# Turning R back by transposes under the query bias, and the sums of x3 taken with its addition

## The chip, the cores and the metric

The program runs on one NeuronCore of a Trainium2 chip. The metric is the device time of one execution in microseconds (us). Engines are named as the profile does: PE is TensorE's matmul stream and PEld its weight loads, DVE is VectorE, ACT is ScalarE, POOL is GpSimd, SP is SyncE (here it issues the DMAs).

## What is computed

The input x has 8 images of 128 x 128 pixels with 32 channels, fp32. Four layers follow each other, each added to its input, each behind a group norm in which every channel of every image is a group of its own:

```python
x = x + _L0_conv_ref(_gn(x), w1, wg, w2)        # per-channel expansion, gelu, 32x32 mixes, gelu, weighting
x = x + _L1_conv_ref(_gn(x), fir)               # 4x4 blur
x = x + _L2_conv_ref(_gn(x), W_qk, b_qk, temp)  # window attention, 8x8 windows
x = x + _L3_conv_ref(_gn(x), W1, b1, gamma, beta)  # involution 3x3, batch norm, leaky relu
```

The change is at the end of the third layer and in the statistics that the fourth one needs:

```python
q = q.reshape(B, WS, H1, WS, W1, HEADS, N)    # queries: a linear map of the window's pixels, N = 64 places
k = k.reshape(B, WS, H1, WS, W1, HEADS, ck)   # keys: 8 channels for each of 4 heads
attn = jnp.einsum('bxyhcp,bxyhdp->bxyhcd', q, k) * temperature   # per window and head: 64 x 8
# attn is laid out again as an 8 x 8 window of 32 channels and added to x (this gives x3)
m = jnp.mean(g, axis=(1, 2, 4)); s = jnp.var(g, axis=(1, 2, 4))  # _gn's moments of x3
```

## The kernel before

The 8 images are worked in two sets of 4 (`NS = 2`), since 4 images x 32 channels fill the 128 partitions. A set's pixels lie in `X` as 128 x 16384 (column w major, row h minor). Each set goes through stages 1 to 4 in turn (the four layers' work up to the moments of x3), then stage 5 follows for the last set and the output for both. At every stage's end `stage_end` makes all five engines wait for each other. The order on each engine's queue is written out by hand, with semaphores between engines.

Stage 4 is the one that changes. Its input is `mall`, the attention matrices M of every window, from stage 3. A *duo* is two columns of windows (16 x 128 pixels of the set, `DUOS = 8` per set), and takes four PSUM banks of 512 columns:

- `r_sum(i)` (L624, TensorE): R, the sum over the input channels of query weights times M, for duo i, into banks 0 to 3. It waits until ScalarE has copied the R of the duo before (`s_rc`).
- the copies (L798, ScalarE): banks 0 to 3 go to `rs[:, i % 2]` in SBUF by two ACTIVATEs of 1024 columns, each raising `s_rc`.
- `r_back(i)` (TensorE): in each of the banks 4 to 7, a product of 32 rows puts down the query bias times the key sums (L646, opens the sum), and four 128 x 128 products of `rs` with the identity turn R back onto it, so that channels are on partitions (L651). Each bank raises `s_xt`. Before it writes bank b of duo i, it waits until VectorE has added that bank of the duo before (`s_x3`).
- VectorE (L1102): `X += bank`, one tensor_tensor for each of the four banks, raising `s_x3`; then `bn_stats` of the same 512 columns (L1093), two per window column.

TensorE's order is `r_sum(0)`, `turn_keys()`, then for every i `r_sum(i + 1)`, `r_back(i)`. `turn_keys` (L632) and two copies by VectorE (L1082) make ready the key sums for the bias. After the last duo VectorE merges the 32 sets of statistics (`moments`, L853 and L854), and GpSimd makes the coefficients of the next group norm from `mv` (L1204 to L1207) and scales the tap weights with them (L1281, L1282), which TensorE's next products (L404, L407) need. On ScalarE a one-column Gelu (L801) stands at the end of the first set's stage. GpSimd does nothing else in stage 4.

## Time and profile before

| | us |
|---|---|
| median of 3 runs (897.27 to 901.45) | 898.84 |
| the profiled execution | 900.62 |
| its span, first to last instruction | 898.7 |
| TensorE matmuls busy | 687.2 (76%) |
| TensorE weight loads busy | 467.2 (52%) |
| VectorE busy | 606.9 (68%) |
| ScalarE busy | 505.4 (56%) |
| GpSimd busy | 265.6 (30%) |
| stage 4 of the first set, first R sum to GpSimd's coefficients | 313.5 to 371.5 |
| stage 4 of the second set | 663.7 to 721.2 |

Busy times overlap, since the engines run side by side, and an engine's idle time costs nothing unless others wait for it. So the table says which engines have room, and the rows by stage say who waits for whom. The granted clock is TensorE's: its two levels are 1.2 and 2.4 GHz, and 1.00 in a row means the upper one throughout.

### The profile page before, as it was taken

Reading aid. Unit: us, or ns where it says so; the run is one execution under the profiler, and the core shown is the slowest. Engines: PE = TensorE matmul, PEld = TensorE weight load, DVE = VectorE, ACT = ScalarE, POOL = GpSimd, SP = SyncE. Lnnn points to the kernel's source line nnn. Section 1 sums busy time; section 2 is a strip of 40 time slices with the busy share of each in tenths; the row PEclk is TensorE's granted clock in tenths of the full one; section 3 lists DMA queues with packets and bytes.
Section 4 is the critical chain, followed back from the end, with each engine's and each line's share of the span. In section 5 each row is a group of like instructions: output and inputs, shape, how many; then the busy total and the mean of one; then the engine's idle time right before and its main releaser. Section 6 shows DMA issues by size and latency. Waiting matters only on the chain. (4 is left out here: it accounts for less than half of the span.)

```text
span 898.7 us, 23273 instructions
## 1 busy us (share of the span) xinstructions
PE 687.2 (76%) x9840; PEld 467.2 (52%) x9840; DVE 606.9 (68%) x1117; ACT 505.4 (56%) x500; POOL 265.6 (30%) x301
## 2 busy tenths in 40 slices
PE   5477776499688799799988659968879988436674
PEld 5322222199666488656311159956658787113443
DVE  4557776699844367556699889954437845968861
ACT  4799999234265433388899614436623100635875
POOL 4511110464055400000000067126510000637863
PEclk9789999799899999899999969979989979657987
DMA  9432220000000000000000000000000000001778
GB/s 307 140 92 83 75 83 25 1 1 1 1 3 4 4 3 2 1 2 1 25 2 1 1 1 2 2 2 3 4 3 3 1 25 1 0 0 51 236 216 246
DMA packets 59910, 37.18 MB, mean 41 GB/s; under 512 B 1952, under 2 KB 59424, under 8 KB 59808
## 3 DMA queue, kind: packets, MB, share of 16 engines
q1 hardware_dynamic: 59808, 35.71, 13.2%
q8 instruction: 78, 1.28, 0.6%
q14 instruction: 24, 0.20, 0.1%
HBM read 18.93 MB, written 16.78 MB: 40 GB/s over the span
## 5 line engine op out<-in xcount | busy, mean ns | idle before, releaser
L728 ACT ACTIVATE work<-X,l0s 128x2048 f32<-128x2048 f32 (+2 forms) x80 | 138.5, 1762 | 16.6 <-POOLq L305 16.6
L743 ACT ACTIVATE work<-ps 128x2048 f32<-128x2048 f32 x64 | 121.0, 1890 | 20.8 <-PE ps L437 20.7
L437 PE MATMUL ps<-work,cst 32*32 32x512 f32 x2048 | 74.3, 606 | 38.5 <-ACT work L743 26.4
L762 ACT ACTIVATE work<-ps 128x512 f32<-128x512 f32 x80 | 47.8, 597 | 92.7 <-PE ps L514 92.7
L525 PE MATMUL ps<-cst,work 128*128 128x143 f32 x640 | 94.8, 293 | 0.4 <-DVE X L1009 0.4
L1204 POOL TENSOR_TENSOR co<-mv,cst 128x1 f32<-128x1 f32 x7 | 1.3, 191 | 317.1 <-DVEq L305 264.3
L525 PEld LDWEIGHTS ps<-cst,work 128*128 128x128 f32 x640 | 86.2, 196 | 1.1 <-issue 1.0
L930 DVE TENSOR_TENSOR X<-X,ps 128x512 f32<-128x512 f32 x64 | 43.7, 683 | 58.3 <-PE ps L450 58.2
L450 PE MATMUL ps<-work,w2d 128*32 128x512 f32 x512 | 70.4, 618 | 2.2 <-ACT work L743 2.2
L798 ACT ACTIVATE work<-ps 128x1024 f32<-128x1024 f32 x32 | 31.0, 1021 | 70.4 <-PE ps L624 70.4
L407 PEld LDWEIGHTS ps<-cst,X 128*128 128x128 f32 x512 | 63.7, 207 | 10.1 <-issue 10.1
L323 POOL TENSOR_SCALAR work<-X,co 128x2048 f32<-128x2048 f32 (+1 forms) x16 | 62.8, 3939 | 20.2 <-PE ps L514 19.8
L1306 POOL TENSOR_TENSOR work<-X,work 128x1024 f32<-128x1024 f32 (+1 forms) x32 | 60.6, 1918 | 21.2 <-ACT work L822 21.2
L514 PE MATMUL ps<-cst,work 128*128 128x128 f32 x320 | 51.0, 284 | 19.7 <-DVE work L1032 19.7
L407 PE MATMUL ps<-cst,X 128*128 128x108 f32 x512 | 65.9, 290 | 0.0
L780 ACT ACTIVATE work<-ps 128x520 f32<-128x520 f32 x64 | 38.7, 605 | 47.1 <-PE ps L574 47.0
L651 PEld LDWEIGHTS ps<-cst,work 128*128 128x128 f32 x512 | 58.4, 192 | 12.1 <-ACT work L798 9.1
L651 PE MATMUL ps<-cst,work 128*128 128x128 f32 x512 | 61.4, 278 | 0.0
L1048 DVE TENSOR_SCALAR work<-X,co 128x1024 f32<-128x1024 f32 x32 | 38.2, 1205 | 33.4 <-PE ps L558 29.6
L1102 DVE TENSOR_TENSOR X<-X,ps 128x512 f32<-128x512 f32 x64 | 42.3, 682 | 24.2 <-PE ps L651 24.2
L1270 POOL TENSOR_TENSOR work<-cst,work 128x256 f32<-128x256 f32 x64 | 58.6, 916 | 0.0
L574 PE MATMUL ps<-work 64*64 64x65 f32 x2048 | 48.7, 229 | 12.3 <-ACT work L780 11.0
(130 smaller groups left out, 1288.5 us busy)
## 6 DMA issues: line engine op xcount, KB each, us to landing
out<-work SPq DMA_DIRECT2D x64, 256.0 KB, 3.2
work<-x SPq DMA_DIRECT2D x16, 512.0 KB, 6.0
work<-x SPq DMA_DIRECT2D x32, 256.0 KB, 2.9
work<-choose SPq DMA_DIRECT2D x8, 128.0 KB, 2.6
cst<-consts SPq DMA_DIRECT2D x1, 1009.5 KB, 9.7
cst<-consts SPq DMA_DIRECT2D x1, 64.0 KB, 1.9
```

Source lines behind the costliest of these rows:

```text
L323: eng.tensor_scalar(strip[:, u, :, lo:hi].rearrange("p h w -> p w h"), X3[:, ds(s * W + t * OW + (lo - 1), hi - lo), :], rstd, nmr, ALU.mu ...
L407: o = pe.matmul(ps[:, 6 + t % 2, j * G * K9:(j + WIDE) * G * K9], X[:, f * PIX + w * H:f * PIX + (w + 1) * H], w9s.rearrange("p (o k) -> p ...
L437: last = pe.matmul(ps[C * m:C * m + C, g, :], wg[rows, m, C * g:C * g + C], y_piece(i, j, m)[rows, :], start=True, stop=True)
L450: last = pe.matmul(ps[C * g:C * g + C, 4 + k % 2, :], w2d[:, :], zb[:, k % ZDEEP, g, :], start=True, stop=True)
L514: last = pe.transpose(ps[:, q, k * P:k * P + P], rows.rearrange("p h w -> p (h w)"), ident)
L525: last = pe.matmul(ps[:, DEEP + 2 * (q % 2) + par, at:at + OW * OH], patch[:, q, k, :], c("fir"), start=True, stop=True)
L574: last = pe.matmul(ps[2 * C * pair:2 * C * pair + 2 * C, 2 + hp, pp * HALF:(pp + 1) * HALF], both[:, 0:2 * C], both, start=True, stop=True)
L651: last = pe.matmul(ps[:, 4 + b, q * P:q * P + P], rs[:, i % RING, 4 * b + q, :], ident, start=False, stop=(q == 3))
L728: act.activation(o, x_in.rearrange("p (j n) -> p j n", n=BANK), ACT.Gelu, scale=l0s[:, at:at + 1], bias=l0s[:, at + MULTI:at + MULTI + 1]) ...
L743: act.activation(zb[:, k % ZDEEP, :, :], ps[:, 0:4, :], ACT.Gelu).then_inc(s_zs, 1)
L1270: pool.tensor_tensor(dx[:, n % SLOTS, :, :, :].rearrange("p a b k -> p (a b) k"), eye, sums.rearrange("p a b o -> p (a b) o").broadcast_to ...
L1306: pool.tensor_tensor(y, group_columns(s, j, b, n), y, ALU.add).then_inc(s_fo, 1)
```

## The change

In `r_back` the transposes come first and open the sum: R is turned by matmuls with `is_transpose=True`, whose output is laid out within a bank by window column j, then window, then row i, so that it matches X's order. The query bias comes second, as the product that closes the sum, with its moving operand in the same order. The four banks are done as two pairs (transposes of two banks, then biases of two banks), and each pair waits for its own copy by ScalarE. VectorE adds a bank with a scalar_tensor_tensor that writes the row sums of the new x3 to `sums`, and its bn_stats are dropped. ScalarE squares x3 minus the mean of x2 (`minus_mean`), 1024 columns at a time, one window column each, and writes the row sums of the squares to `squares`; the squares themselves go to a scratch (`squared`). Each square waits for VectorE's two additions and for the square before it. In ScalarE's order the two squares of duo i - 1 stand behind the copies of duo i, and the last two at the end. At the stage's end `totals` replaces the merge of the statistics: two reductions and four small steps on VectorE give mean and variance. Nothing of the computation is left out.

```diff
--- before.py
+++ after.py
@@ -105,6 +105,7 @@
         w2d = sb("w2d", C)
         head_of, place_of = sb("head_of", HEADS), sb("place_of", WS)
         tap = sb("tap", 2 * G * K9)
+        sums, squares, tot = sb("sums", NB), sb("squares", NB), sb("tot", 4)
         ps = ctx.enter_context(nc.psum_tensor("ps", [P, 8, BANK], fp32))
 
         X3 = X[:, :].rearrange("p (w h) -> p w h", h=H)
@@ -177,6 +178,8 @@
         bias_q, _e = part(_e, [WS, N])
         ksum = work[:, _e:_e + NWIN * NWIN]
         assert _e + 2 * NWIN * NWIN <= WORK
+        squared = work[:, _e + NWIN * NWIN:_e + NWIN * NWIN + 2 * BANK]
+        assert _e + NWIN * NWIN + 2 * BANK <= WORK
 
         U, _e = part(0, [3, W, G])
         T, _e = part(_e, [TB + 2, G * K9])
@@ -266,6 +269,8 @@
         s_rc = sem("r_copied")
         s_xt = sem("r_transposed")
         s_x3 = sem("x3_written")
+        s_sq = sem("squares_summed")
+        s_tot = sem("total_step")
         s_sel = sem("sel_loaded")
         s_sc = sem("s_spread")
         s_v = [rsem("even_v_ready", "dve"), rsem("odd_v_ready", "pool")]
@@ -639,18 +644,20 @@
                     if i == 0:
                         pe.wait_ge(s_bq, s + 1)
                         pe.wait_ge(s_kl, s + 1)
-                    for b in range(4):
-                        if nn:
-                            pe.wait_ge(s_x3, 4 * nn - 3 + b)
-                        rows = slice(C * b, C * b + C)
-                        pe.matmul(ps[:, 4 + b, :], turned_k[rows, i, :], bias_q[rows, :, :].rearrange("p w n -> p (w n)"),
-                                  start=True, stop=False)
-                    pe.wait_ge(s_rc, 2 * nn + 2)
-                    for b in range(4):
-                        for q in range(4):
-                            last = pe.matmul(ps[:, 4 + b, q * P:q * P + P], rs[:, i % RING, 4 * b + q, :], ident,
-                                             start=False, stop=(q == 3))
-                        last.then_inc(s_xt, 1)
+                    for pair in range(2):
+                        pe.wait_ge(s_rc, 2 * nn + pair + 1)
+                        for b in range(2 * pair, 2 * pair + 2):
+                            if nn:
+                                pe.wait_ge(s_x3, 4 * nn - 3 + b)
+                            by_pixel = ps[:, 4 + b, :].rearrange("p (j q i) -> p q j i", j=WS, i=WS)
+                            for q in range(4):
+                                pe.matmul(by_pixel[:, 2 * q:2 * q + 2, :, :], rs[:, i % RING, 4 * b + q, :], ident,
+                                          start=(q == 0), stop=False, is_transpose=True)
+                        for b in range(2 * pair, 2 * pair + 2):
+                            rows = slice(C * b, C * b + C)
+                            pe.matmul(ps[:, 4 + b, :], turned_k[rows, i, :],
+                                      bias_q[rows, :, :].rearrange("p w (j i) -> p j w i", j=WS),
+                                      start=False, stop=True).then_inc(s_xt, 1)
 
                 r_sum(0)
                 turn_keys()
@@ -789,6 +796,15 @@
                 stage_end(act, s, 3)
 
 
+                def square_x3(w1):
+
+                    at = s * PIX + w1 * WS * H
+                    act.wait_ge(s_x3, s * NB + 2 * w1 + 2)
+                    if w1:
+                        act.wait_ge(s_sq, s * NWIN + w1)
+                    act.activation(squared, X[:, at:at + WS * H], ACT.Square, bias=minus_mean,
+                                   accum_out=squares[:, w1:w1 + 1]).then_inc(s_sq, 1)
+
                 for i in range(DUOS):
                     nn = s * DUOS + i
                     act.wait_ge(s_r, nn + 1)
@@ -797,6 +813,11 @@
                     for j in range(0, 4, 2):
                         act.activation(rs[:, i % RING, 4 * j:4 * j + 8, :].rearrange("p m k -> p (m k)"),
                                        ps[:, j:j + 2, :].rearrange("p j k -> p (j k)"), ACT.Copy).then_inc(s_rc, 1)
+                    if i:
+                        square_x3(2 * i - 2)
+                        square_x3(2 * i - 1)
+                square_x3(NWIN - 2)
+                square_x3(NWIN - 1)
                 if s + 1 < NS:
                     act.activation(warm[:, 1:2], warm[:, 0:1], ACT.Gelu)
                 stage_end(act, s, 4)
@@ -852,6 +873,29 @@
             def moments(n):
                 dve.drain()
                 dve.bn_aggr(mv[:, :], stats[:, 0:6 * n]).then_inc(s_aggr, 1)
+
+            steps_t = [0]
+
+            def totals(n1, n2, minus_c):
+
+                def step(ins):
+                    ins.then_inc(s_tot, 1)
+                    steps_t[0] += 1
+
+                def stepped():
+                    dve.wait_ge(s_tot, steps_t[0])
+                    alone(dve)
+
+                step(dve.tensor_reduce(tot[:, 0:1], sums[:, 0:n1], mybir.AxisListType.X, ALU.add))
+                step(dve.tensor_reduce(tot[:, 1:2], squares[:, 0:n2], mybir.AxisListType.X, ALU.add))
+                stepped()
+                dve.tensor_scalar(mv[:, 0:1], tot[:, 0:1], 1.0 / PIX, None, ALU.mult)
+                step(dve.tensor_scalar(tot[:, 2:3], tot[:, 0:1], 1.0 / PIX, minus_c, ALU.mult, ALU.add))
+                stepped()
+                step(dve.tensor_tensor(tot[:, 3:4], tot[:, 2:3], tot[:, 2:3], ALU.mult))
+                stepped()
+                dve.scalar_tensor_tensor(mv[:, 1:2], tot[:, 1:2], 1.0 / PIX, tot[:, 3:4], ALU.mult, ALU.subtract
+                                         ).then_inc(s_aggr, 1)
 
             dve.wait_ge(s_ident, 16)
             by_head = ident.rearrange("p (g h k) -> p h g k", g=G, h=HEADS)
@@ -1087,22 +1131,15 @@
                     def half_windows(hf):
                         return X3[:, ds(s * W + w1 * WS, WS), 64 * hf:64 * hf + 64]
 
-                    def measure_x3(hf):
-                        dve.wait_ge(s_x3, s * NB + w1 * 2 + hf + 1)
-                        alone(dve)
-                        dve.bn_stats(stats[:, 12 * w1 + 6 * hf:12 * w1 + 6 * hf + 6], half_windows(hf))
-
-                    def windows(hf):
-                        return half_windows(hf).rearrange("p j (q i) -> p j q i", i=WS)
-
-
                     for hf in range(2):
                         dve.wait_ge(s_xt, s * NB + w1 * 2 + hf + 1)
-                        src = ps[:, 4 + 2 * (w1 % 2) + hf, :].rearrange("p (q j i) -> p j q i", j=WS, i=WS)
-                        dve.tensor_tensor(windows(hf), windows(hf), src, ALU.add).then_inc(s_x3, 1)
-                    measure_x3(0)
-                    measure_x3(1)
-                moments(NB)
+                        v = half_windows(hf)
+                        dve.scalar_tensor_tensor(v, v, 1.0, ps[:, 4 + 2 * (w1 % 2) + hf, :].rearrange("p (j h) -> p j h", j=WS),
+                                                 ALU.mult, ALU.add, accum_out=sums[:, 2 * w1 + hf:2 * w1 + hf + 1]
+                                                 ).then_inc(s_x3, 1)
+                dve.wait_ge(s_x3, (s + 1) * NB)
+                dve.wait_ge(s_sq, (s + 1) * NWIN)
+                totals(NB, NWIN, minus_mean)
                 stage_end(dve, s, 4)
                 if s + 1 < NS:
                     continue
```

## Rows read from the trace of the kernel before

**Rows 1.** Page of the kernel: busy time of TensorE and of others, granted clock in 40 slices.

```profile
PE 687.2 (76%) x9840; PEld 467.2 (52%) x9840; DVE 606.9 (68%) x1117; ACT 505.4 (56%) x500; POOL 265.6 (30%) x301
PEclk9789999799899999899999969979989979657987
```

**Rows 2.** Chain of waits, second set's stage 4: start us, us, what.

```profile
673.61 1.14 PE ps L624 x63
674.74 1.36 PE ps L646 x8
676.10 3.77 PE ps L651 x32
...
711.19 2.49 PE ps L646 x8
```

**Rows 3.** Windows, one duo: length, busy per engine, PEclk, DMA share, GB/s.

```profile
337.51:343.77 6.26, 6.26 (x109) 5.21 (x104) 4.95 (x9) 1.94 (x2) 0.00 (x0) 1.00 0.00 0
```

**Rows 4.** Timeline, the same duo: start us, us, engine, line, idle before.

```profile
337.62 1.94 ACT L798 ACTIVATE work<-ps 128x1024 f32<-128x1024 f32 x2 [4.32 <-PE ps L624]
...
338.87 3.84 PE L651 MATMUL ps<-cst,work 128*128 128x128 f32 x32
340.06 0.69 DVE L1102 TENSOR_TENSOR X<-X,ps 128x512 f32<-128x512 f32 x1 [1.10 <-PE ps L651]
```

**Rows 5.** L646's rows running from 361.9 to 362.1; timeline of weight loads.

```profile
L646 PE MATMUL ps<-work x4: 587/640/692, 361.4 to 362.0; 32*128 32x512 f32 x4
...
362.87 0.29 PEld L646 LDWEIGHTS ps<-work 32*128 32x128 f32 x2 [0.31 <-DVE X L1102]
363.92 0.19 PEld L651 LDWEIGHTS ps<-cst,work 128*128 128x128 f32 x1 [0.76 <-issue]
```

**Rows 6.** Timeline of TensorE where it transposes; windows as above.

```profile
885.70 1.98 PE L694 MATMUL ps<-cst,work 128*128 128x128 f32 x16 [0.29 <-ACT work L833]
...
23.10 1.09 PE L395 MATMUL ps<-cst,work 128*128 128x128 f32 x8 [0.34 <-POOL work L1218]
...
22.00:27.00 5.00, 3.85 (x31) 3.08 (x29) 4.52 (x8) 4.56 (x8) 3.67 (x4) 1.00 1.02 321
```

**Rows 7.** Groups by line and shape: count, busy us, mean ns, idle before.

```profile
L814 ACT ACTIVATE work<-X,co 128x512 f32<-128x512 f32 x16 | 11.5, 721 | 67.3 <-PE ps L317 56.6 <-DVE stats L1119 10.7
L728 ACT ACTIVATE work<-X,l0s 128x1536 f32<-128x1536 f32 x16 | 26.8, 1678 | 0.0
L728 ACT ACTIVATE work<-X,l0s 128x512 f32<-128x512 f32 x16 | 13.2, 824 | 0.0
L801 ACT ACTIVATE warm<-warm 128x1 f32<-128x1 f32 x1 | 0.2, 206 | 0.0
L719 ACT ACT_TABLE_LOAD x1 | 1.3, 1283 | 9.1 <-DVE stats L850 9.1
L1171 DVE SCALAR_TENSOR_TENSOR work<-X,vall,ps 128x512 f32<-128x512 f32 x64 | 43.6, 743 | 15.0 <-PE ps L317 15.0
```

**Rows 8.** Timeline, first bias, last turns and the end of stage 4.

```profile
668.70 1.14 PE L646 MATMUL ps<-work 32*128 32x512 f32 x8
...
713.61 3.84 PE L651 MATMUL ps<-cst,work 128*128 128x128 f32 x32
...
721.15 0.19 POOL L1204 TENSOR_TENSOR co<-mv,cst 128x1 f32<-128x1 f32 x1 [58.52 <-DVEq L305]
```

**Rows 9.** Timeline of VectorE's dependent one-column steps ahead of the output.

```profile
799.85 0.16 DVE L1151 TENSOR_REDUCE bns<-ps 128x1 f32<-128x2 f32 x1 [1.57 <-PE ps L681]
...
800.50 0.16 DVE L1154 TENSOR_TENSOR bns<-bns 128x2 f32<-128x2 f32 x1
```

**Rows 10.** Timeline and windows where TensorE runs at the lower clock.

```profile
313.57 2.27 PE L624 MATMUL ps<-work,cst 32*64 32x128 f32 x64 [2.64 <-SPq L368]
...
7.14 6.34 PEld L395 LDWEIGHTS ps<-cst,work 128*128 128x128 f32 x32 [7.14 <-issue]
...
313.50:316.00 2.50, 2.43 (x65) 2.13 (x66) 0.00 (x0) 0.12 (x1) 0.00 (x0) 0.50 0.03 7
```

## The prediction

> **What bounds the kernel now.** I first looked for where each engine is full. Over the span no engine is (TensorE is busy 76%), so the question is what the touched stage, stage 4 of either set, waits for [rows 1]. The chain of waits answers it: through this stage it never leaves TensorE. Each duo (two strips of windows, four PSUM banks) costs three links: 1.14 us for the sums of R (L624), 1.36 us for the four bias products (L646), 3.77 us for the sixteen turns (L651), together 6.27 us, six times over between 673.61 and 711.19 in the second set [rows 2]. The stretch of one duo says the same: TensorE busy 6.26 of 6.26 us at full granted clock, VectorE 4.95, ScalarE 1.94 [rows 3]. The timeline shows why nothing else matters: ScalarE ends its copies 4.32 us before the next sums, and VectorE idles 1.10 us for the turns [rows 4]. So TensorE time taken out of a duo is time off the end, until another engine is longer; at 4.95 us VectorE would be next, unless its work shrinks too.
>
> **TensorE, part by part.** A turn is now a product with the identity, issued as two instructions: sixteen turns are 32 matmuls in 3.84 us, so (3.84 - 0.275)/31 = 0.115 us from one to the next [rows 4]. Transposes in this trace are one instruction each: sixteen in 1.98 us with a last one of 0.273 us, which is 1.71/15 = 0.114 us; eight in 1.09 us, 0.117 us [rows 6]. I take 0.115: sixteen turns become 1.84 us, 1.93 us less per duo.
>
> The output of the new transposes lies in runs of eight elements 64 apart, which no transpose of the trace does. The nearest row is L624, which writes such runs: 32 products on eight tiles of the array at once, four rounds in 1.14 us, 0.285 us each, against 0.235 us (3.77/16) for a contiguous product of as many columns [rows 2]. So the factor lies between 1.0 and 1.21; I take 1.0, because most of L624's excess can as well be its 64 small weight loads. The upper end adds 16 x 0.115 x 0.21 = 0.39 us per duo. The Trainium skill speaks against this part (PSUM — Partial Sum Buffer, Specifications (TRN2): access patterns that aren't contiguous slow matmuls significantly). It gives no figure; L624's row speaks against a factor of two.
>
> The bias products lose company. Four banks in four row groups ran together in 1.36 us; now they come two at a time. The last duo prices that, since its products waited for VectorE: two started together at 361.4, their second halves at 362.0; the last bank came alone at 362.87, and the first turn's weights loaded at 363.92, 1.05 us later [rows 5]. A pair starts 0.02 us apart, so 1.07 us a pair, 2.14 us a duo, 0.78 us more than now. Bounds: 0.95 if the pair's end overlaps the next loads, 1.36 if a pair costs what four do.
>
> New duo: 1.14 + 1.84 + 2.14 = 5.12 us against 6.27.
>
> **ScalarE.** It gains two squares of 1024 columns per duo. A 512-column ACTIVATE from SBUF with a pointer bias takes 0.722 us; the growth from 512 to 1536 columns is (1678 - 824)/1024 = 0.834 ns a column, so 1.15 us for 1024 [rows 7]. Writing the sum out isn't in the trace: between 0 and 0.21 us (the one-column ACTIVATE), I take 0.15, in the middle since it is a step of its own but needn't be a whole ACTIVATE. ScalarE per duo: 1.94 + 2 x 1.30 + about 0.1 for the waits = 4.65 us, under 5.12. Square may want a table load, 1.28 us [rows 7]; Copy, Identity and Prelu run on the loaded table without one, so I take 0, at most two loads per set.
>
> What is queued behind the squares matters more than their sum. The copies of duo i+2 stand behind the squares of duo i, and the sums of duo i+3 on TensorE wait for those copies. From the end of duo i's turns: 0.1 to VectorE, two additions 1.48, 0.06, one square 1.30, two copies 1.94, 0.05, together 4.93 us; TensorE meanwhile does one duo, 5.12 us. Hidden, with 0.2 us to spare. The reordering itself makes banks 0 and 1 complete half a duo earlier, so the first square of a duo isn't late.
>
> **VectorE.** 64 bn_stats of 0.682 us leave. The additions become three-operand instructions with a sum: 0.74 us is the same form with PSUM input (L1171) [rows 7]; with the sum's read-out (0 to 0.16 us, the one-column reduction of [rows 9]) 3.0 to 3.6 us per duo instead of 4.95. Off the path either way. The Trainium skill (VectorE: DVE Perf Modes, Two Vector instructions with no wait between them) says that an accumulator output makes an instruction two; no row here shows one, and the sum doesn't need it.
>
> **End of the stage.** Before, from the last turn's end (717.45) to GpSimd's start (721.15): 3.70 us of additions, stats and their aggregate [rows 8]. After: 0.1 + 1.48 (additions) + 0.06 + 1.30 (last square) + 0.06 + totals + 0.09. Totals are two reductions and then dependent small steps; four such steps run from 799.85 to 800.66, 0.81 us [rows 9], and with the two extra small ones I take 1.1 (0.9 to 1.4). Sum 4.19 us: 0.5 us lost per set.
>
> **The sum.** TensorE from the first bias product (668.70) to the last turn's end: 48.75 us per set [rows 2, 8]. After: six sums of R and eight duos' turns and biases, 6 x 1.14 + 8 x 3.98 = 38.7 us, and the wait of 1.13 us for VectorE in the last bias group (2.49 against 1.36 [rows 2]) is gone, since the additions of banks 2 and 3 now have a pair's time, 2 us. Gain 10.0 - 0.5 = 9.5 us per set, 19.0 in two. The profiled execution took 900.62 us (span 898.7), so 881.6; it lies 1.8 us above the median of the three runs, 898.84, and against that I get 879.8, said as 880.
>
> **Rivals.**
> ScalarE becomes the bound. If the read-out and the step between waiting squares cost 0.6 us each instead of 0.2, ScalarE needs about 1.94 + 2 x 1.75 + 0.1 = 5.5 us a duo: 16 x 0.4 = 6.4 us back, 886. For: the sum's price is unknown and the loop above has only 0.2 us to spare. Against: no small row on ScalarE is over 0.21 us. 0.17.
>
> The turns don't get cheaper. If scattered output or accumulation holds a transpose at the 0.235 us of a product (or the flag doesn't make it one pass), a duo is 1.14 + 3.77 + 2.14 = 7.05 us; per set 6.84 + 8 x 5.91 = 54.1 against 48.75, plus 0.5 at the end: 5.9 x 2 = 11.8 slower, 911. It decides from 0.19 us per turn, where (48.75 - 0.5 - 6.84 - 8 x 2.14)/128 = 0.19 us breaks even. For: pairs of biases surely cost more. Against: every transpose of the trace runs at 0.115. 0.07.
>
> The clock falls. At the lower level sums of R took 2.27 us at a granted clock of 0.50, and the first 32 transposes 6.34 us, 0.198 each [rows 10]; with biases at twice their time a duo is 2.27 + 3.17 + 4.28 = 9.7 us, 74 us more in all, 954. Against: from 22 to 27 us TensorE did transposes alone, with gaps of 0.35 us, at clock 1.00 and 0.273 us apiece [rows 6], and here it has no gaps. The Trainium skill has the rule behind this rival (TensorE: Matmul & The Clock Gate, Part 4: transposes don't count as busy, so full rate doesn't engage). The trace disagrees. 0.02.
>
> TensorE overlaps more than I allow: pairs of 0.95 us and the next loads under them give 0.24 us per duo more, 876 or, with cheaper transposes, 874. 0.06.
>
> **How the numbers follow.** The forecast has 0.68: 880, by itself 876 to 884. Low end: 7 us below, the overlap rival with the shortest totals. High end: ScalarE-bound 886 plus part of the 0.39 us per duo for scattered output, 888. Outside lie the two slow rivals and a corner where pairs cost 1.36, about 0.12. 0.5% is 4.5 us, about what a measurement of this kernel can tell from no change. Faster: forecast, ScalarE and overlap, 0.91; within: 0.02, where several upper bounds meet; slower 0.07 (turns 0.05, clock 0.02; the rest of the turns' chance is partial and falls within).
>
> **What would show it.** Right: 16 TensorE instructions per duo in place of 32 with about 0.115 us between them; biases in pairs 1.07 us apart from the next load; a duo period of 5.1; the chain on TensorE; VectorE about 3 us a duo; GpSimd starting its coefficients 9 to 10 us earlier after the first bias. Wrong: TensorE waiting for L798's copies (ScalarE or the loop), a period that doesn't shrink, table loads next to squares, or a granted clock under 1 in the stage.

## The result, and the profile after

| | kernel before | changed kernel |
|---|---|---|
| median | 900.67 us (897.27 to 903.5, 7 runs) | 891.31 us (886.83 to 894.59, 7 runs) |
| profiled execution, its span | 900.62, 898.7 | 886.83, 885.0 |
| stage 4, first and second set | 57.9, 57.4 | 49.7, 49.2 |
| the output | 100.2 | 101.7 |

The ratio of the medians is 0.9892, with a 95% interval of 0.9862 to 0.9922. So the change makes the kernel 9.4 us faster, where the prediction said 19; 891.3 lies above the range (873 to 888). Stage 4 gave most of what was forecast for it, 16.4 of 19.0 us. The rest was lost outside it, in stages that the change doesn't touch. The profiled execution of the changed kernel is the fastest of its seven, so its profile shows less of that loss than the medians. The stage lengths in this text run from the first sum of R to GpSimd's coefficients, and the output from GpSimd's first step (L1330 in the changed kernel) to the end of the span.

The page after, answering [rows 1]: TensorE lost 256 instructions and 18.3 us of busy time, VectorE 39.2, and ScalarE gained 38.3.

```profile
PE 668.9 (76%) x9584; PEld 433.5 (49%) x9584; DVE 567.7 (64%) x1127; ACT 543.7 (61%) x564; POOL 265.8 (30%) x301
PEclk9879999889989999799999969979999989557987
```

The chain of waits through one duo of the second set and the end of the stage, answering [rows 2, 8]; the columns are start, us, and what:

```profile
667.12 1.14 PE ps L629 x63
668.26 1.02 PE ps L654 x8
669.28 1.06 PE ps L658 x4
670.34 1.02 PE ps L654 x8
671.36 1.06 PE ps L658 x4
672.42 1.14 PE ps L629 x63
...
702.01 1.11 PE ps L658 x4
703.11 1.30 DVE X L1137 x4
704.43 1.15 ACT work L805
...
707.16 0.19 POOL co L1241
```

L629 are the sums of R, L654 the turns, L658 the biases. Nothing but TensorE stands between two sums, and a duo takes 672.42 - 667.12 = 5.30 us. Two stretches inside stage 4 of either set, answering [rows 3] (length, busy of PE, PEld, DVE, ACT, POOL, granted clock, DMA share, GB/s):

```profile
322.00:340.00 18.00, 18.00 (x297) 11.00 (x303) 9.16 (x29) 13.87 (x19) 0.00 (x0) 1.00 0.01 2
665.00:703.00 38.00, 38.00 (x566) 23.07 (x564) 19.56 (x60) 28.98 (x41) 0.00 (x0) 1.00 0.01 2
```

TensorE is busy without a gap at the full clock; VectorE is at half, ScalarE at three quarters. And the timeline of a duo of the first set, answering [rows 4]:

```profile
321.73 1.09 PE L654 MATMUL ps<-cst,work 128*128 128x128 f32 x8
321.83 0.69 DVE L1137 SCALAR_TENSOR_TENSOR X<-X,ps 128x512 f32<-128x512 f32 x1 [2.58 <-PE ps L658]
322.44 0.08 DVE L1137 DVE_READ_ACCUMULATOR X<-X,ps 128x1 f32 x1
322.44 0.68 DVE L1137 SCALAR_TENSOR_TENSOR X<-X,ps 128x512 f32<-128x512 f32 x1
322.75 1.13 PE L658 MATMUL ps<-work 32*128 32x512 f32 x4
...
325.25 1.15 ACT L805 ACTIVATE work<-X,co 128x1024 f32<-128x1024 f32 x1 [0.84 <-DVE X L1137]
...
326.30 0.19 ACT L805 ACTIVATION_READ_ACCUMULATOR work<-X,co 128x1 f32 x1
```

The additions follow each other every 0.61 us, with a read-out of 0.08 us of their own; a square takes 1.15 us and its read-out 0.19. The turns run at full speed, one every 0.115 us, but the first bias comes 1.02 us after the first of eight turns (322.75 - 321.73), and not after 8 x 0.115 = 0.92.

### The profile page after: what moved, and what is told of

Same layout as the page of the kernel before. It is cut to its first block and busy times, and to the rows that moved or that the text cites. A ratio compares the mean times of both kernels' runs of the same rounds, so it can differ in the third digit from the quotient of the medians.

```text
span 885.0 us, 22837 instructions
## 1 busy us (share of the span) xinstructions
PE 668.9 (76%) x9584; PEld 433.5 (49%) x9584; DVE 567.7 (64%) x1127; ACT 543.7 (61%) x564; POOL 265.8 (30%) x301
## 5 line engine op out<-in xcount | busy, mean ns | idle before, releaser
L442 PE MATMUL ps<-work,cst 32*32 32x512 f32 x2048 | 76.4, 623 | 37.7 <-ACT work L750 26.4
L530 PEld LDWEIGHTS ps<-cst,work 128*128 128x128 f32 x640 | 86.0, 196 | 0.7 <-issue 0.7
L974 DVE TENSOR_TENSOR X<-X,ps 128x512 f32<-128x512 f32 x64 | 43.7, 683 | 59.1 <-PE ps L455 59.1
L787 ACT ACTIVATE work<-ps 128x520 f32<-128x520 f32 x64 | 38.7, 605 | 49.5 <-PE ps L579 49.4
L1137 DVE SCALAR_TENSOR_TENSOR X<-X,ps 128x512 f32<-128x512 f32 x64 | 41.5, 685 | 41.9 <-PE ps L658 41.9
L519 PE MATMUL ps<-cst,work 128*128 128x128 f32 x320 | 51.2, 285 | 19.7 <-DVE work L1076 19.7
L1307 POOL TENSOR_TENSOR work<-cst,work 128x256 f32<-128x256 f32 x64 | 57.9, 905 | 0.0
L1047 DVE TENSOR_TENSOR X<-X,ps 128x286 f32<-128x286 f32 (+1 forms) x120 | 52.8, 440 | 6.4
L563 PE MATMUL ps<-cst,work 128*128 128x128 f32 x256 | 44.7, 302 | 14.4 <-DVE work L1092 14.4
L579 PEld LDWEIGHTS ps<-work 64*64 64x64 f32 x2048 | 40.5, 138 | 30.3 <-issue 30.1
```

Of the source, the lines that this page charges most:

```text
L442: last = pe.matmul(ps[C * m:C * m + C, g, :], wg[rows, m, C * g:C * g + C], y_piece(i, j, m)[rows, :], start=True, stop=True)
L519: last = pe.transpose(ps[:, q, k * P:k * P + P], rows.rearrange("p h w -> p (h w)"), ident)
L530: last = pe.matmul(ps[:, DEEP + 2 * (q % 2) + par, at:at + OW * OH], patch[:, q, k, :], c("fir"), start=True, stop=True)
L579: last = pe.matmul(ps[2 * C * pair:2 * C * pair + 2 * C, 2 + hp, pp * HALF:(pp + 1) * HALF], both[:, 0:2 * C], both, start=True, stop=True)
L1047: last = dve.tensor_tensor(v, v, src[:, 0:ow], ALU.add)
L1307: pool.tensor_tensor(dx[:, n % SLOTS, :, :, :].rearrange("p a b k -> p (a b) k"), eye, sums.rearrange("p a b o -> p (a b) o").broadcast_to ...
```

## The experiments

Line numbers in the profiles are those of each kernel, shifted by one or a few. Unless told otherwise a kernel leaves out nothing. The first four runs split the change in its parts.

**The change and the kernel before, unedited.**

> The changed kernel, unedited, for a second profile of it. In the first profile stage 4 lost 8.2 us per set (57.9 and 57.4 us before, 49.7 and 49.2 after, first sums of R to GpSimd's coefficients), 16.4 in all, yet the medians lie only 9.4 us apart and the profiled executions 13.8. Theory A (the rest lies outside stage 4): stage 4 takes 49.2 to 49.7 us again in a slower execution, at granted clock 1.00 through the duos, and what is late is another stage; time 0.986 to 0.993 of before. Theory B (the clock in stage 4): in a typical execution the clock falls within stage 4, a duo takes more than 5.30 us somewhere, and stage 4 is 52 to 56 us.

> The kernel before, unedited, against itself. Both theories: ratio 1.000 within 0.003, stage 4 57.4 to 57.9 us. If theory A holds, its other stages differ between this profile and the first one by as much as 2 to 5 us in all; if nothing outside stage 4 moves between two executions, under 1 us, theory A needs another ground.

Measured: 888.61 us (881.44 to 889.92), ratio 0.9873 (0.9836 to 0.9909); and 897.28, ratio 0.9993 (0.9972 to 1.0014). Stage 4 of the second profile of the change took again 49.2 and 49.6 us, its output again 101.7, where that of the second profile of before took 97.4. So theory A holds: stage 4 keeps its gain in a slower execution, and the loss lies outside it.

**TensorE's part alone.** The change's `r_back`, with tensor_tensor and bn_stats on VectorE and no squares:

```diff
-                        dve.scalar_tensor_tensor(v, v, 1.0, ps[:, 4 + 2 * (w1 % 2) + hf, :].rearrange("p (j h) -> p j h", j=WS),
-                                                 ALU.mult, ALU.add, accum_out=sums[:, 2 * w1 + hf:2 * w1 + hf + 1]
-                                                 ).then_inc(s_x3, 1)
+                        dve.tensor_tensor(v, v, ps[:, 4 + 2 * (w1 % 2) + hf, :].rearrange("p (j h) -> p j h", j=WS), ALU.add
+                                          ).then_inc(s_x3, 1)
+                    measure_x3(0)
+                    measure_x3(1)
```

> The change's TensorE part alone: transposes first, bias on top, two banks at a time, addition without sums; bn_stats and their merge on VectorE as before, no squares on ScalarE. Theory 1 (TensorE sets the period, so the statistics' move brings nothing): VectorE needs 8 x 0.64 = 5.1 us of a duo, under TensorE's 5.30, so a duo stays at 5.30, the end of the stage is 0.4 us shorter than with the squares, and stage 4 takes 48.9 us: as fast as the whole change, 0.985 to 0.993 of before. Rival 2 (VectorE, with its order of two additions and two bn_stats, holds the banks up): a duo at 5.5 to 5.8 us, stage 4 51 to 53 us, 0.99 to 0.996.

Measured: 889.14 us, ratio 0.9885 (0.9851 to 0.9918), stages 4 of 50.0 and 49.7 us. So TensorE's part makes up the change; with the new statistics a set is another 0.1 to 0.8 us shorter.

**The statistics alone.** The products of before in their order, output laid out by pixel, and the change's sums and squares. One line of it, against the kernel before:

```diff
-                            last = pe.matmul(ps[:, 4 + b, q * P:q * P + P], rs[:, i % RING, 4 * b + q, :], ident,
+                            last = pe.matmul(by_pixel[:, 2 * q:2 * q + 2, :, :], rs[:, i % RING, 4 * b + q, :], ident,
```

> The change's statistics alone: sums with the addition, squares on ScalarE; on TensorE the order and the products of before (bias first, four banks, 32 turn instructions), only written by pixel row as the addition with a sum needs it. Theory 1: TensorE's duo stays 6.27 us, the end of the stage grows 0.4 us per set, so time is 1.000 to 1.002 of before. Rival 3 (a product written in runs of eight elements is slower): a turn above 0.235 us, a duo of 6.5 to 7 us, ratio 1.005 to 1.013.

Measured: 894.4 us, ratio 0.9957 (0.9927 to 0.9987), stages 4 of 55.4 and 54.9 us, 2.5 us shorter than before in either set though the same products run; neither theory had this. Its chain:

```profile
686.07 1.14 PE ps L629 x63
687.21 1.07 PE ps L651 x8
688.28 3.77 PE ps L657 x32
```

The four biases take 1.07 us here, not the 1.36 of [rows 2]. The chain of the kernel before has this price too, at the set's first duo, where the additions that the biases wait for are long done:

```profile
668.77 1.07 PE ps L646 x8
```

The timeline of before two duos later says why (VectorE's statistics L1093, additions L1102; weight loads and matmuls of the biases L646):

```profile
679.33 0.68 DVE L1093 BATCH_NORM_STATS2 stats<-X 128x6 f32<-128x512 f32 x1
...
679.92 1.27 DVE L1102 TENSOR_TENSOR X<-X,ps 128x512 f32<-128x512 f32 x2
680.94 0.60 PEld L646 LDWEIGHTS ps<-work 32*128 32x128 f32 x8 [0.17 <-issue]
```

The statistics of banks 0 and 1 hold back the additions of banks 2 and 3; these end at 679.92 + 1.27 = 681.19, while the biases began at 680.94. The fourth bias waits for them, and the loads of the four are spread over 0.60 us; in the kernel with the statistics alone they take 0.31. The row showed a product where 0.29 us of it was a wait.

**Four banks at a time.** If four biases cost what two do, splitting them in pairs costs a whole pair:

```diff
-                    for pair in range(2):
-                        pe.wait_ge(s_rc, 2 * nn + pair + 1)
-                        for b in range(2 * pair, 2 * pair + 2):
+                    pe.wait_ge(s_rc, 2 * nn + 2)
+                    for b in range(4):
...
-                        for b in range(2 * pair, 2 * pair + 2):
+                    for b in range(4):
...
```

> The changed kernel with four banks at a time: sixteen transposes, then the four bias products together. In the run with the statistics alone four bias products took 1.07 us when nothing waited, as long as a pair, so the split into pairs should cost TensorE one group per duo. Theory 1 (the pairs only cost time): TensorE needs 1.14 + 2.04 + 1.07 = 4.25 us, ScalarE 1.94 + 2 x 1.34 = 4.6 us, a duo takes 4.6 us and stage 4 44 us, 10 us less in two sets than with pairs. Rival (the pairs are needed for the loop through ScalarE): the additions of all four banks come after the last product, so from the turns' end to the sums two duos on it is 0.1 + 2.6 + 0.06 + 1.35 + 1.94 + 0.05 = 6.1 us; with TensorE's 4.25 that is 10.35 for two duos, 5.2 us each, and stage 4 stays at 48.5 to 50 us.

Measured: 880.67 us, ratio 0.9827 (0.9775 to 0.988), stages 4 of 47.9 and 47.6, near the rival's 48.5 to 50. The chain leaves TensorE (L1136 additions, L804 squares, L813 copies, L629 sums of R, L653 turns):

```profile
673.66 1.30 DVE X L1136 x4
...
674.98 1.25 ACT work L804 x2
...
678.37 1.02 ACT work L813
...
679.43 1.21 PE ps L629 x63
680.64 1.90 PE ps L653 x16
```

This is a longer form of the prediction's loop through ScalarE: the additions begin only after all four biases, the copies stand behind both squares and not one, and the sums of R wait for the copies. The sums of R reached this way start at 669.45, 679.43 and 689.42, two duos apart, so a duo takes 4.99 us.

**The same with the squares a duo later** in ScalarE's order:

```diff
-                    if i:
-                        square_x3(2 * i - 2)
-                        square_x3(2 * i - 1)
+                    if i > 1:
+                        square_x3(2 * i - 4)
+                        square_x3(2 * i - 3)
...
```

> Four banks at a time and the squares of a duo one duo later in ScalarE's queue, so that the copies never stand behind additions just made. If the loop of b1's rival is what holds, it is gone here: ScalarE's own work of 4.6 us sets the duo, 8 x 0.7 us less than the change per set, but four squares instead of two are left at the stage's end (2.7 us more at most); stage 4 takes 45 to 47.5 us, 4 to 8 us less in two sets than the change. If the loop isn't it, b1 and b2 take the same time per duo.

Measured: 872.62 us, ratio 0.9709 (0.9674 to 0.9745), stages 4 of 44.1 and 43.6; in a later group 872.08 (below). It beats both kernels. The chain is TensorE's rows again, 4.32 us a duo, less than the 4.6 that was expected of ScalarE:

```profile
654.87 1.90 PE ps L653 x16
...
662.16 1.14 PE ps L629 x63
663.30 2.12 PE ps L653 x16
665.41 1.07 PE ps L657 x8
666.49 1.14 PE ps L629 x63
```

But the sixteen turns, 1.90 us in the first duo, take 2.12 in the later ones, and the timeline shows a late partner here too: the last four turns wait until VectorE has added the fourth bank of the duo before.

```profile
669.08 0.42 PEld L653 LDWEIGHTS ps<-cst,work 128*128 128x128 f32 x4 [0.19 <-DVE X L1136]
```

So the duo is set by the loop of four biases, four additions and four turns, with 0.2 us of wait in it. ScalarE, busy 20.5 of 22 us from 658 to 680, is near its end as well.

**Four banks at a time with bn_stats on VectorE** and no squares:

> Four banks at a time with the TensorE part alone: bn_stats stay on VectorE. Theory 1 (the statistics' move is worth something only once TensorE's duo is below VectorE's 5.1 us): VectorE sets the duo at 5.1 us against 4.32 with late squares on ScalarE (b2), so stage 4 takes 48 us, near b1's 47.7, and 4 us more than b2's 43.8. Rival (VectorE's second pair of additions stands behind two bn_stats and holds the banks): a duo of 5.5 us or more, stage 4 51 us.

Measured: 894.97 us, ratio 0.995 (0.9926 to 0.9974), stages 4 of 53.4 and 54.1. VectorE isn't full (it idles 0.60 us a duo, waiting for the biases), but it holds the banks: the additions of the last two banks stand behind two bn_stats, and the last eight turns wait for them. This is the rival of the expectation. The biases start at 680.32, 685.79 and 691.26 in the chain, 5.47 us apart:

```profile
685.79 1.11 PE ps L657 x8
686.90 0.73 DVE X L1136 x2
...
688.68 0.68 DVE stats L1131
...
690.00 1.25 PE ps L653 x8
691.26 1.11 PE ps L657 x8
```

So the new statistics are worth 0.4 us a set with pairs, 2.5 with the order of before, and 5.5 to 6.4 once TensorE does all four banks together.

**Turns as products**, in the change:

```diff
-                                          start=(q == 0), stop=False, is_transpose=True)
+                                          start=(q == 0), stop=False)
```

> The changed kernel with its turns as plain products with the identity, written to the same places; everything else as in the change. Theory 1 (one-pass transposes are the whole gain, pairs cost one bias group): a turn 0.235 us, a duo 1.14 + 2 x (1.88 + 1.05) = 7.0 us, stage 4 63 us per set, ratio to before 1.010 to 1.016. Rival (the gain is mostly the relief of VectorE): a duo under 6.27 us and a ratio under 1.

Measured: 913.82 us, ratio 1.0173 (1.0129 to 1.0217), stages 4 of 65.1 and 64.6. Eight turns take 1.98 us with the step to the biases, and the duo 1.14 + 2 x (1.98 + 1.06) = 7.22, so the first theory holds, a little above its numbers:

```profile
681.31 1.14 PE ps L629 x63
682.45 1.98 PE ps L654 x16
684.43 1.06 PE ps L658 x4
```

**TensorE's part with contiguous output**, VectorE reading the banks in the old order:

```diff
-                                pe.matmul(by_pixel[:, 2 * q:2 * q + 2, :, :], rs[:, i % RING, 4 * b + q, :], ident,
+                                pe.matmul(flat[:, q * P:q * P + P], rs[:, i % RING, 4 * b + q, :], ident,
```

> As the TensorE part alone (a3), but the transposes and the bias write a bank in the order of before, contiguous per transpose, and VectorE reads it in that order. Theory 1 (output in runs of eight costs nothing): eight transposes and what follows take 1.02 us as in a3, a duo 5.30 us, stage 4 49.7 to 50 us. Rival (scattered writes slow a transpose): 0.92 us for eight, a duo 5.1 us, stage 4 48.1 us.

Measured: 889.1 us, ratio 0.9888 (0.9856 to 0.9921), as with scattered output (889.14). The chain shows the same two lengths, so the runs of eight cost nothing:

```profile
671.89 1.02 PE ps L654 x8
672.91 1.06 PE ps L658 x4
```

**Pauses on GpSimd.** What was left is the time outside stage 4. The median less both stages 4 is 782.5 to 785.4 us for the kernel before and its repeat and 784.1 to 785.2 for statistics alone, four banks, late squares and turns as products, but 792.4 and 789.8 for the change and 788.3 to 789.4 for TensorE's part (four banks with bn_stats lie between, 787.5): against the kernel before beside them, 6 to 7 us more for the change and 3 to 7 for the others, in code that is the same. Either this code's length depends on when it starts (placement), or the difference is chance or something that stage 4 leaves behind, and a pause would only add itself. Three runs put a pause ahead of GpSimd's coefficients at the end of the second stage 4:

```diff
+                    if s and k == 3:
+                        for n in (1024, 400):
+                            pool.memset(squared[:, 0:n], 0.0)
+                            pool.drain()
                     normal(mv)
```

> The changed kernel with a pause: GpSimd clears a scratch ahead of the coefficients at the end of the second set's stage 4, about 1.3 us in which everyone waits. In ten profiles the output stage takes 97.3 to 97.4 us where the granted clock rises 23.0 to 23.2 us after its start (five kernels, none of them the change), 101.7 where it rises at 22.0 to 22.2 (the change twice, its TensorE part alone) and 105.7 at 21.3. Theory C (where stage 5 starts against the points at which the clock can change is set by how long stage 4 took, and decides the output's mode): the pause moves it to where the faster kernels are; output 97.4 us in the profile, and the median is 0.5 to 3 us lower than the change's in spite of the pause, ratio to before 0.981 to 0.986. Theory D (the modes fall by chance): output any of the values, and the median 1.3 us higher, ratio 0.989 to 0.991.

> As c1, with a pause of about 2.6 us. Theory C: the output's time depends on the pause and not evenly; with 2.6 us the kernels seen so far give no neighbour, so any of 97.4 to 105.7, but the same in most executions. Theory D: median 2.6 us above the change's, ratio 0.990 to 0.993, the profile any of the values.

> The kernel before with a pause of about 2.4 us at the same place. Theory C: it is put where the change stands, so its output takes 101.7 us or more in the profile and its median rises by 2.4 and about 4 more, ratio 1.005 to 1.008. Theory D: ratio 1.0027, within its interval.

(The first of these texts counts five kernels with an output of 97.4 us. Of the ten profiles four had it, and two, before and late squares, took 100.2.)

Six more runs belong together. Five put memsets of 384 columns ahead of the output's first step, so that stages 1 to 5 stay as they were; in the change five and three of them, in the kernel before three, in the one with late squares one and five. The sixth is late squares without a pause. The edit of the first:

```diff
+            for _p in range(5):
+                pool.memset(stats[:, 0:384], 0.0)
+                pool.drain()
             pool.tensor_tensor(bns[:, 0:2], va[:, 0, :], va[:, 2, :], ALU.mult).then_inc(s_g, 1)
```

> The change with a pause of about 2.4 us on GpSimd ahead of the first step of the output (five memsets of a tile that nobody reads any more), stage 4 and everything up to the output untouched; nothing is left out. In the change the output took 101.7 us and TensorE's granted clock rose to full 22.0 to 22.2 us after its start; where the rise came at 23.0 to 23.2 the output took 97.4 us. Theory (the output's length hangs on where its start falls against the clock's rise): the output, counted from its own start after the pause, is not 101.7 us long any more; if the rise comes at 23 us it is 97.4, and the kernel is 2.4 - 4.3 = 1.9 us faster than the unedited change, about 888. Rival (the output's 101.7 us come from something stage 4 leaves behind, its shorter length or its data, and a pause is only added): 101.7 stays and the time is 2.4 us more, about 892.

> The kernel before with a pause of about 1.4 us at the same place, three memsets; nothing is left out. Its outputs took 97.4 to 100.2 us with the rise at 23.0 to 23.5 us after the start. Theory: the rise comes 1.4 us earlier against the start, at about 22, which went with 101.7 us in the change; so 1.4 + 1.5 to 4.3, that is 3 to 6 us slower than the kernel before, ratio 1.003 to 1.006. Rival (a pause is only added): 1.4 us, ratio 1.0015, the output 97.4 to 100.2.

> As the first of this group with a pause of about 1.4 us. Theory: the rise moves from 22.0 to 22.2 us after the start to 20.7, or to a later place; at 21.3 the output took 105.7 in one kernel. So anything but 101.7 with 1.4 us added is for it, most likely a slower kernel, about 894. Rival: 1.4 us more than the unedited change, output 101.7.

> Four banks at a time with the squares a duo later (the fastest kernel so far, its output 100.2 us with the rise at 23.5 us after the start), and a pause of about 0.5 us ahead of the output, one memset; nothing is left out. Theory: the rise comes at 23.0 and the output takes 97.4, so 0.5 - 2.8 = 2.3 us faster than without the pause, about 870. Rival: 0.5 us slower, 873.

> Four banks at a time with the squares a duo later, unedited, for comparison in one group with the pause of 0.6 us (879.75 us in the group before) and with the next kernel. If placement is what matters, it repeats near 872.6 us and the pause of 0.6 us did cost 7 us; if it now takes 878 or more, that cost was the chip's day.

> The same with a pause of about 2.7 us ahead of the output, five memsets; nothing is left out. Theory of placement: the cost is not in proportion to the pause. 0.6 us cost 7 us with the rise of the clock 21.5 us after the output's start; in the change a pause of 2.7 us took the rise to 22 us and an output of 101.8, so here 2.7 + 1.6 = 4.3 us, about 877, below the 879.75 of the shorter pause. Rival (a pause costs itself and something fixed for being there): 2.1 us above the shorter pause, 882.

Measured, with the pause as its row has it (for instance, in the kernel before: `L1294`, where the next step starts 0.14 us behind the row's end):

```profile
798.47 1.50 POOL L1294 MEMSET stats<- 128x384 f32 x3 [2.56 <-DVEq L305]
800.11 0.19 POOL L1296 TENSOR_TENSOR bns<-vall 128x2 f32<-128x2 f32 x1
```

| kernel | pause | median | ratio (95%) | output in its profile |
|---|---|---|---|---|
| before, in stage 4 | 2.75 | 907.02 | 1.0075 (1.0051 to 1.0099) | 101.6 |
| before, ahead of the output | 1.50 | 908.15 | 1.0078 (1.005 to 1.0106) | 105.8 |
| change, in stage 4 | 1.50 | 887.4 | 0.986 (0.9833 to 0.9887) | 97.4 |
| change, in stage 4 | 2.91 | 892.4 | 0.9912 (0.9883 to 0.9941) | 101.8 |
| change, ahead of the output | 1.50 | 887.34 | 0.9849 (0.9802 to 0.9896) | 104.9 |
| change, ahead of the output | 2.57 | 888.79 | 0.9858 (0.9805 to 0.9911) | 101.8 |
| late squares, none | 0 | 872.08 | 0.9739 (0.9703 to 0.9775) | 97.4 |
| late squares, ahead of the output | 0.42 | 879.75 | 0.9749 (0.9698 to 0.98) | 104.8 |
| late squares, ahead of the output | 2.57 | 881.3 | 0.9801 (0.977 to 0.9832) | 106.0 |

The pauses of 1.5 and 2.75 us cost the kernel before 7.6 and 7.8 us against the runs of before beside them (900.57 and 899.21). The one of 2.57 us cost late squares 9.2 us against the same kernel in the same group; that of 0.42 us 7 us by the medians, but it ran in another group, and its ratio (0.9749 against 0.9709 and 0.9739) doesn't make this certain. The change with three of its pauses came out between 4 us under and level with its own two medians (888.6 and 891.3), with the longest 1 to 4 us over. A theory in which a pause only adds its length gives the last of these, but none of the others. Placement said two of the runs ahead, the kernel before with a pause in stage 4 (output 101.6 and ratio 1.0075, where 101.7 and 1.005 to 1.008 were said) and the change with the short pause there (97.4, and 0.986 at the edge of 0.981 to 0.986). The others it could not: late squares with the shortest pause were said to be 2.3 us faster and came slower, with the longer pause 877 was said and 881 came, the change's output stayed at 101.8 where 97.4 was hoped for (though its median, 888.8, is near the 888 said), the change with three memsets had an output of 104.9 us but not the 894 said, and the kernel before with the pause ahead of the output lost more than the 3 to 6 us said. A profile is one execution, too: that of the change with 1.50 us ahead of the output took 894.06, and the median was 887.3.

What holds in every profile shows when all 20 are put in the order of the time from the output's start to the rise of TensorE's granted clock from 0.50 to 1.00, read from windows of half a microsecond:

| clock rises after | output | profiles |
|---|---|---|
| 21.2 to 21.8 us | 104.8 to 105.8 us | 4: TensorE's part with flat output, three with a pause |
| 22.0 to 22.2 | 101.6 to 101.8 | 6: both of the unedited change, TensorE's part alone, three with a pause |
| 22.6 to 23.4 | 97.3 to 97.4 | 7: second of before, statistics alone, turns as products, four banks (both statistics), change with the short pause in stage 4, second of late squares |
| 23.5 | 100.2 | 2: first of before, first of late squares |
| 24.0 | 106.0 | 1: late squares with the longer pause |

The first column doesn't order the lengths: the latest rise went with the longest output. What orders them is the clock behind the rise. These are windows of the output's work from 25 to 75 us after its start, one profile for each kind: before again (output 97.4), before (100.2), the change (101.7), before with a pause ahead of the output (105.8), late squares with the longer pause (106.0):

```profile
822.33:872.33 50.00, 33.58 (x264) 22.27 (x264) 41.99 (x57) 43.35 (x34) 43.22 (x23) 1.00 0.75 223
823.49:873.49 50.00, 35.47 (x256) 25.04 (x256) 40.38 (x54) 40.66 (x32) 41.51 (x22) 0.93 0.72 215
808.27:858.27 50.00, 34.67 (x246) 24.45 (x247) 39.69 (x54) 40.92 (x33) 40.00 (x21) 0.92 0.71 210
825.11:875.11 50.00, 36.22 (x240) 26.14 (x240) 35.67 (x50) 38.27 (x30) 37.79 (x20) 0.86 0.69 205
800.04:850.04 50.00, 35.62 (x228) 26.61 (x229) 36.37 (x50) 38.39 (x30) 37.22 (x20) 0.83 0.64 192
```

After the rise the clock stays up in the first and falls back again and again in the others, to means of 0.93, 0.92, 0.86 and 0.83, and in the same 50 us TensorE does 264, 256, 246, 240 and 228 matmuls. All 20 profiles agree: 1.00 in the seven of 97.3 to 97.4 us, 0.93 in the two of 100.2, 0.91 or 0.92 in the six of 101.6 to 101.8, 0.86 in the four of 104.8 to 105.8, 0.83 in that of 106.0. The order of the output's work is the same in all. So the length of the output goes with the clock granted in it; which of these courses the clock takes went with the time of the rise in every profile, but why isn't known.

## Why the prediction missed

**Stage 4: mechanism right, size short.** The step that was mis-sized is the new duo of 5.12 us; it took 5.30. The two turns of eight were priced as a flow (8 x 0.115 = 0.92) without the step from turns to biases; they took 1.02 each, 0.2 us a duo. The sum's 38.7 us for six sums of R and eight duos' turns and biases becomes 6 x 1.14 + 8 x 4.16 = 40.1. The end took 4.05 us from the last bias (703.11) to GpSimd (707.16), where 4.19 was said. So 10.0 - 1.4 - 0.4 = 8.2 us a set, as measured (57.9 to 49.7, 57.4 to 49.2), 2.6 us less than forecast in two sets. The medians then split as 19.0 - 2.6 - 7.0 = 9.4, with 7.0 us lost outside stage 4.

**All else stays: wrong.** This assumption stood in the sum without a word: it took the time of the profiled execution and subtracted stage 4's gain. Between the two profiled executions little was lost outside (13.8 us gained of 16.4), but in the medians only 9.4. In the profiles taken the second time it is 7.5 of 16.0 (spans 894.7 and 887.2). The largest part is the output: the clock rose 22.0 to 22.2 us after its start in both profiles of the change, 23.1 and 23.5 in those of before, and it took 1.5 to 4.3 us more. Stage 1 of the second set was 149.8 and 150.5 us long against 148.5 and 149.1. The stretch between the two stages 4, the same code in all, took 292.5 to 295.6 us in the six profiles of the change, with or without a later pause, and 291.2 to 293.3 in the four of before. The stage 5 ahead of the output came out at 76.1 and 79.1 against 77.3 and 77.0. Single profiles differ by as much without any change: the code ahead of the first stage 4 is the same in all 20, and it ended between 311.0 and 316.1 us.

That a shift can move the time by this much is shown by the pauses: the kernel before, shifted by 1.5 to 2.75 us, lost over 7 us by the medians, 5 to 6 us more than the pause. That the change's 6 to 7 us are all of this kind is not shown: with the pause that gave its output 97.4 us in the profile its median was 887.4, only 1.2 to 3.9 us less, or 2.7 to 5.4 less without the 1.50 us of the pause itself. What makes the clock fall back in the output wasn't tried, and why the medians of the change differ by 2.7 us between groups stays open.

**Turns.** 0.115 us apiece and a factor of 1.0 for scattered output: right; contiguous output has the same 1.02. The Trainium skill (PSUM — Partial Sum Buffer, Specifications (TRN2)) says that access patterns that aren't contiguous slow matmuls significantly; for runs of eight fp32 these two kernels disagree.

**Biases.** A pair was said at 1.07 us and took 1.06. But the 1.36 of [rows 2] for four was taken for work, and so was the 0.78 us that pairs were to cost; four cost 1.07, and pairs cost 2 x 1.06 - 1.07 = 1.05 us and a second handover. The bound "1.36 if a pair costs what four do" named the right case with the wrong number. Hence the kernel with four banks at a time, 8 to 11 us under the change.

**VectorE "off the path either way".** In the kernel before it was on it, as a wait inside a row of TensorE: without it a set of the order of before is 2.5 us shorter (six duos of 0.29, 0.6 in the last bias group, the rest at the end). The additions took 0.61 us from one to the next with a read-out of 0.08, 2.6 us a duo (2 x 1.30) instead of 3.0 to 3.6. The read-out has a row of its own, as the Trainium skill has it (VectorE: DVE Perf Modes, Two Vector instructions with no wait between them): an accumulator output makes an instruction two.

**ScalarE.** Square 1.15 us as said, its read-out 0.19 (0.15 taken, 0 to 0.21 the bounds), no table load beside the two that the kernel before has too. The loop of 4.93 us under 5.12 stayed hidden, since the duo was 5.30. Its longer form set the duo, at 4.99, in the kernel with four banks, whose TensorE needs only some 4.2 us (1.21 + 1.90 + 1.11).

**Rivals.** ScalarE as the bound: not in the change, where it was busy three quarters; in four banks at a time the loop through it held, not its read-outs. Turns no cheaper: the kernel with turns as products is that case, 913.8 against the 911 said; 7.22 us a duo against 7.05. The clock in stage 4: 1.00 in the two stretches above, with turns for 2.04 of a duo's 5.30 us. The price of this rival was misread: the first 32 transposes of [rows 10], 0.198 us each, ran at a granted clock of 1.00 from 7 to 13 us, not at the lower level. The Trainium skill (TensorE: Matmul & The Clock Gate, Part 4) says that transposes don't count as busy. Stage 4 can't test that, since other products fill the other 3.26 us of a duo; [rows 6] disagrees. More overlap: the opposite came.

## What to carry to other kernels

A row of the chain of waits can hold a wait: where several instructions of one row take longer than the same instructions elsewhere (1.36 against 1.07 us for four biases, 2.12 against 1.90 for sixteen turns here), look on the timeline for the late partner before pricing a split of them. Price a change of kind on TensorE (turns to biases, 0.1 us each time) as well as the instructions, and do few of them: four banks at a time with the squares moved behind the next copies gave 872.6 us where pairs gave 889 to 891. And where TensorE's granted clock falls between stages, a small shift can change the course of the clock in a later stage, so a forecast within 1% of such a kernel needs 5 to 7 us of range for that alone (what the pauses cost two kernels beyond their own length), and a test of two versions should see each with a pause or two.

## What the runs showed of the hardware

- The output, the same work each time, took 97.3 to 106.0 us in 20 profiles, in step with TensorE's mean granted clock from 25 to 75 us after its start: 97.4 us at 1.00, 100.2 at 0.93, 101.7 at 0.92, 104.8 to 105.8 at 0.86, 106.0 at 0.83. The time of the rise went with it, but not in order: 97.4 at 23.4 us, 100.2 at 23.5, 106.0 at 24.0, 101.7 at 22.1.
- Four row-tiled products of 32 x 512 fp32 on four banks take 1.07 us, two take 1.06.
- A sum written with the instruction costs VectorE a row of 0.08 us, hidden between additions 0.61 us apart, and ScalarE one of 0.19 us.
- A transpose flagged as such takes 0.115 us in fp32 also when it is written in runs of eight and opens a sum that a product closes; unflagged, as a product, it takes 0.235 ((1.98 - 0.10)/8, 0.10 being the step to the biases).
